# Third stage of a two-layer decoder: GpSimd's products four heads at a time, and VectorE's order around the sums of values and the cross attention's row addition

## The reference

```python
def _L1_attn_ref(x, wq, wk, wv, wo, sink):          # rope, band of 64, 16 heads on 4 key heads
    ...
def _L1_xattn_ref(q, k, v, Wq, bq, Wk, bk, Wv, bv, Wo, bo):
    Q = (q @ Wq.T + bq).reshape(bs, sl, H, HD)       # H = 16 heads of HD = 16
    K = (k @ Wk.T + bk).reshape(bs, sl, H, HD)
    V = (v @ Wv.T + bv).reshape(bs, sl, H, HD)
    score = jnp.einsum('bshd,bsgd->bshg', Q, K)
    weight = jax.nn.softmax(score, axis=-1)
    attn = jnp.einsum('bshg,bsgd->bshd', weight, V).reshape(bs, sl, nf)
    return attn @ Wo.T + bo
def _L1_ffn_ref(hidden_states, ln1_w, ln2_w, Wq, Wk, Wv, Wo, A, B, W_in_base, W_up_base, W_down):
    mod = MOD_SCALE * jnp.tanh(_attention(rmsnorm(h, ln1_w)) @ A)      # causal, 16 heads
    gate_pre = h @ W_in_base.T + mod * (h @ A) @ B                     # h = rmsnorm(hidden, ln2_w)
    return residual + (silu(gate_pre) * (h @ W_up_base.T)) @ W_down.T
```

## Time and profile before

| what | value |
|---|---|
| median of three runs | 3036.44 us |
| the profiled execution, its own time | 3033.89 us |
| its span from first to last instruction | 3032.2 us |
| busy over the span: PE / DVE / ACT / POOL | 2750.8 / 2487.2 / 1954.2 / 2111.9 us |
| third stage, first gather to the end | about 1940 to 3032 us |
| steady turns of the third stage | 24, from 2164.9 to 2885.8 us |
| products q-k, 512 instructions | 358.9 us, 743 ns each |
| products weights-values, 512 instructions | 369.5 us, 760 ns each |

### The profile page before, as it was taken

The page is one execution under the profiler, slowest core; times in us unless marked ns, Lnnn a source line. Parts: engine busy times, 40 slices in busy tenths (PEclk is TensorE's granted clock), DMA queues, the critical chain, the costliest instruction groups (busy, mean ns, idle before and its releaser), DMA issues. The chain is left out here.

```text
span 3032.2 us, 68140 instructions
## 1 busy us (share of the span) xinstructions
PE 2750.8 (91%) x22096; PEld 2295.9 (76%) x22128; DVE 2487.2 (82%) x5452; ACT 1954.2 (64%) x4120; POOL 2111.9 (70%) x2651
## 2 busy tenths in 40 slices
PE   6999999999999999999788499667999999999978
PEld 3888888888888888888555299535777777777767
DVE  6888888888888888888599577468899898989863
ACT  5888878778787877878444155346666666666642
POOL 5897666666666666666468544369888989898870
PEclk9999999999999999999899699768999999999989
DMA  4555444444444444444444399600000000000000
GB/s 144 172 193 169 133 143 139 144 135 146 137 131 153 131 143 132 155 131 128 142 152 146 134 337 333 207 15 18 20 19 27 21 25 24 22 24 22 21 5 11
DMA packets 185881, 340.09 MB, mean 112 GB/s; under 512 B 40668, under 2 KB 104037, under 8 KB 178936
## 3 DMA queue, kind: packets, MB, share of 16 engines
q1 hardware_dynamic: 179448, 319.55, 32.6%
q0 software_dynamic: 6144, 16.79, 1.8%
HBM read 264.68 MB, written 63.19 MB: 108 GB/s over the span
## 5 line engine op out<-in xcount | busy, mean ns | idle before, releaser
L1804 POOL TENSOR_TENSOR l_prod<-l_sco,l_kv 128x256 f32<-128x256 f32 x512 | 369.5, 760 | 36.4 <-DVE l_sco L2311 36.4
L1797 POOL TENSOR_TENSOR l_prod<-l_q,l_kv 128x256 f32<-128x256 f32 x512 | 358.9, 743 | 47.3 <-DVE l_att L2319 47.3
L718 DVE SCALAR_TENSOR_TENSOR a_cq<-a_PQ,a_taps,a_cq 128x504 f32<-128x504 f32 (+2 forms) x384 | 281.7, 734 | 72.7 <-ACT a_cq L584 63.6
L718 DVE SCALAR_TENSOR_TENSOR a_ck<-a_PK,a_taps,a_ck 128x504 f32<-128x504 f32 (+2 forms) x384 | 280.6, 731 | 9.7 <-ACT a_ck L584 0.5
L342 POOL TENSOR_TENSOR a_tq<-a_cq,a_tq 128x512 f32<-128x512 f32 x128 | 165.9, 1296 | 131.2 <-ACT a_tq L590 131.1
L329 POOL TENSOR_TENSOR a_hrs<-a_hve,a_neghalf 128x8 f32<-128x8 f32 x128 | 209.6, 1638 | 25.7 <-DVE a_hve L735 25.2
L485 PE MATMUL a_Y<-a_wo,a_og_parts 128*128 128x256 f32 x1536 | 205.9, 284 | 5.0 <-POOL a_og_parts L336 5.0
L412 PEld LDWEIGHTS a_X<-a_wv,a_xb 128*128 128x128 f32 x1536 | 200.0, 188 | 12.1 <-issue 1.2
L342 POOL TENSOR_TENSOR a_tk<-a_ck,a_tk 128x512 f32<-128x512 f32 x128 | 163.6, 1278 | 62.8 <-ACT a_tk L590 62.8
L412 PE MATMUL a_PQ<-a_x_hi,a_wqk 128*128 (+1 forms) x512 | 194.1, 420 | 12.6 <-issue 11.9
L412 PE MATMUL a_X<-a_wv,a_xb 128*128 128x256 f32 x1536 | 204.2, 282 | 0.8 <-DMA a_xb<-a_x_lo 0.8
(11 more groups left out here) (398 smaller groups left out, 8380.6 us busy)
## 6 DMA issues: line engine op xcount, KB each, us to landing
a_wqk<-qk_parts SPq DMA_DIRECT2D x112, 512.0 KB, 3.4
m_wgu<-gate_up_parts SPq DMA_DIRECT2D x39, 1024.0 KB, 8.1
a_wv<-v_parts SPq DMA_DIRECT2D x56, 512.0 KB, 3.8
a_wg<-g_parts SPq DMA_DIRECT2D x112, 256.0 KB, 3.3
a_wo<-o_parts SPq DMA_DIRECT2D x112, 256.0 KB, 2.9
a_dr<-decays SPq DMA_DIRECT2D x256, 64.0 KB, 2.6
m_hs<-sorted_rows SPq DMA_DIRECT2D x39, 256.0 KB, 7.1
sorted_outs<-m_ys SPq DMA_DIRECT2D x39, 256.0 KB, 7.5
```

The costliest lines, as they stand in the source:

```text
L718: nc.vector.scalar_tensor_tensor(out=acc, in0=src, scalar=taps[p][:, tap + k:tap + k + 1], in1=acc, op0=ALU.mult, op1=ALU.add).then_inc(s_ ...
L1797: nc.gpsimd.tensor_tensor(out=prod[:, h], in0=qv[:, h:h + 1, :].to_broadcast([P, H, HD]), in1=kk, op=ALU.mult).then_inc(S("E_pqk"), 1)
L1804: nc.gpsimd.tensor_tensor(out=prod[:, h], in0=sco[:, h:h + 1, :].to_broadcast([P, HD, H]), in1=vv, op=ALU.mult).then_inc(S("E_pav"), 1)
```

## The change

Three things change in the third stage, and nothing in the first two.

1. products_qk and products_av issue four instructions of 128 x 1024 (four heads) instead of sixteen of 128 x 256. One operand is broadcast over the last heads' axis, as before, and the other one over the four heads. The counts of E_pqk and E_pav follow (4 per tile instead of 16).
2. gather passes the row numbers straight from slots to the indirect DMA; the copy into of_tile, the two small operations and their semaphores are gone.
3. VectorE's list: f_x2lo and E's statistics stand behind the last sum of values; sums 2 and 1 of values stand ahead of m_hidden(1); et_x stands in the next turn, behind the first score sum and ahead of F's arguments.

The core of the diff:

```diff
             def load_kv(t):
                 if t >= 3:
-                    sp.wait_ge(S("E_pav"), H * (t - 2))
+                    sp.wait_ge(S("E_pav"), 4 * (t - 2))
...
-                for h in range(H):
-                    nc.gpsimd.tensor_tensor(out=prod[:, h], in0=qv[:, h:h + 1, :].to_broadcast([P, H, HD]), in1=kk,
-                                            op=ALU.mult).then_inc(S("E_pqk"), 1)
+                for k in range(4):
+                    heads = slice(4 * k, 4 * k + 4)
+                    nc.gpsimd.tensor_tensor(out=prod[:, heads], in0=qv[:, heads, :].unsqueeze(2).to_broadcast([P, 4, H, HD]),
+                                            in1=kk.unsqueeze(1).to_broadcast([P, 4, H, HD]), op=ALU.mult).then_inc(S("E_pqk"), 1)
...
-                for h in range(H):
-                    nc.gpsimd.tensor_tensor(out=prod[:, h], in0=sco[:, h:h + 1, :].to_broadcast([P, HD, H]), in1=vv,
-                                            op=ALU.mult).then_inc(S("E_pav"), 1)
+                for k in range(4):
+                    heads = slice(4 * k, 4 * k + 4)
+                    nc.gpsimd.tensor_tensor(out=prod[:, heads], in0=sco[:, heads, :].unsqueeze(2).to_broadcast([P, 4, HD, H]),
+                                            in1=vv.unsqueeze(1).to_broadcast([P, 4, HD, H]), op=ALU.mult).then_inc(S("E_pav"), 1)
...
             def gather(t):
-                wait_if(pool, S("G_ready"), 2 * t)
                 wait_if(pool, S("G_x"), 2 * t)
-                nc.gpsimd.tensor_tensor(out=ready[:], in0=neghalf[:, 0:1], in1=neghalf[:, 0:1], op=ALU.mult).then_inc(S("G_ready"), 1)
-                nc.gpsimd.tensor_copy(of_tile[:], slots[:, tile(t), :].rearrange("p t k -> p (t k)")).then_inc(S("G_at"), 1)
...
-                                                 bass.IndirectOffsetOnAxis(ap=of_tile[:, k:k + 1], axis=0)).then_inc(S(f"G_in{k}"), 16)
+                                                 bass.IndirectOffsetOnAxis(ap=slots[:, t, k:k + 1], axis=0)).then_inc(S(f"G_in{k}"), 16)
...
-            iterate(dve, [("Et", et_scores(0)), ("Ft", arguments("F")), ("F", statistics("F", "E_x", 1)), ("Et", et_scores(2)),
+            iterate(dve, [("Et", et_scores(0)), ("F", et_x), ("Ft", arguments("F")), ("F", statistics("F", "E_x", 1)), ("Et", et_scores(2)),
...
```

More of the change, by code:

```diff
@@ L1666, in layer_one @@
         got = [sb(f"got{k}", [P, D]) for k in range(2)]
-        of_tile, ready = sb("of_tile", [P, 2], mybir.dt.uint32), sb("ready", [P, 1])
         xT = {k: sb("xT" + k, [P, DC, P]) for k in "DF"}
@@ L1802, in products_av @@
                 vv = kv[t % 3][:, 1, :].rearrange("p (d g) -> p d g", d=HD)
-                for h in range(H):
-                    nc.gpsimd.tensor_tensor(out=prod[:, h], in0=sco[:, h:h + 1, :].to_broadcast([P, HD, H]), in1=vv,
-                                            op=ALU.mult).then_inc(S("E_pav"), 1)
+                for k in range(4):
+                    heads = slice(4 * k, 4 * k + 4)
+                    nc.gpsimd.tensor_tensor(out=prod[:, heads], in0=sco[:, heads, :].unsqueeze(2).to_broadcast([P, 4, HD, H]),
+                                            in1=vv.unsqueeze(1).to_broadcast([P, 4, HD, H]), op=ALU.mult).then_inc(S("E_pav"), 1)
             def gather(t):
-                wait_if(pool, S("G_ready"), 2 * t)
                 wait_if(pool, S("G_x"), 2 * t)
-                nc.gpsimd.tensor_tensor(out=ready[:], in0=neghalf[:, 0:1], in1=neghalf[:, 0:1], op=ALU.mult).then_inc(S("G_ready"), 1)
-                nc.gpsimd.tensor_copy(of_tile[:], slots[:, tile(t), :].rearrange("p t k -> p (t k)")).then_inc(S("G_at"), 1)
-                pool.wait_ge(S("G_ready"), 2 * t + 1)
-                pool.wait_ge(S("G_at"), t + 1)
-                nc.gpsimd.tensor_tensor(out=ready[:], in0=neghalf[:, 0:1], in1=neghalf[:, 0:1], op=ALU.mult).then_inc(S("G_ready"), 1)
                 for k in range(2):
                     nc.gpsimd.indirect_dma_start(got[k][:], None, outs[:, :],
-                                                 bass.IndirectOffsetOnAxis(ap=of_tile[:, k:k + 1], axis=0)).then_inc(S(f"G_in{k}"), 16)
+                                                 bass.IndirectOffsetOnAxis(ap=slots[:, t, k:k + 1], axis=0)).then_inc(S(f"G_in{k}"), 16)
             pool.wait_ge(S("masked"), 4)
@@ L2077, in e_q @@
             def e_q(t):
-                wait_if(act, S("E_pqk"), H * t)
+                wait_if(act, S("E_pqk"), 4 * t)
                 act.wait_ge(S("E_qp"), t + 1)
@@ L2292, in piece @@
                 def piece(t):
-                    wait_if(dve, S("E_pav"), H * t)
-                    dve.wait_ge(S("E_pqk"), H * t + 4 * k + 4)
+                    wait_if(dve, S("E_pav"), 4 * t)
+                    dve.wait_ge(S("E_pqk"), 4 * t + k + 1)
                     nc.vector.reduce_sum(sco[:, 4 * k:4 * k + 4, :], prod[:, 4 * k:4 * k + 4], axis=AX).then_inc(S("E_sc"), 1)
@@ L2317, in piece @@
                     wait_if(dve, S("E_aTp"), t)
-                    dve.wait_ge(S("E_pav"), H * t + 4 * k + 4)
+                    dve.wait_ge(S("E_pav"), 4 * t + k + 1)
                     nc.vector.reduce_sum(att[:].rearrange("p (h d) -> p h d", d=HD)[:, 4 * k:4 * k + 4, :], prod[:, 4 * k:4 * k + 4],
@@ L2385, in _ @@
             dve.wait_ge(S("masked"), 4)
-            iterate(dve, [("Et", et_scores(0)), ("Ft", arguments("F")), ("F", statistics("F", "E_x", 1)), ("Et", et_scores(2)),
+            iterate(dve, [("Et", et_scores(0)), ("F", et_x), ("Ft", arguments("F")), ("F", statistics("F", "E_x", 1)), ("Et", et_scores(2)),
                           ("Et", et_scores(1)), ("Et", et_scores(3)), ("Et", et_shift), ("Dt", divide("D", EB)), ("Et", et_weights),
                           ("M", m_hidden(0)), ("D", d_rope), ("Dn", combine), ("Et", et_values(0)), ("Ft", divide("F", MI)),
-                          ("Dn", statistics("D", "G_x", 2)), ("F", f_x2lo), ("Dt", d_x), ("M", m_hidden(1)),
-                          ("En", statistics("E", "D_x", 1)), ("Et", et_values(2)), ("Et", et_values(1)), ("Ft", ft_gm),
-                          ("Et", et_values(3)), ("D", arguments("D")), ("Ft", ft_gm_lo), ("Md", m_x), ("Et", et_x), ("Et", split_low)])
+                          ("Dn", statistics("D", "G_x", 2)), ("Dt", d_x), ("Et", et_values(2)), ("Et", et_values(1)), ("M", m_hidden(1)),
+                          ("Et", et_values(3)), ("F", f_x2lo), ("En", statistics("E", "D_x", 1)), ("Ft", ft_gm),
+                          ("D", arguments("D")), ("Ft", ft_gm_lo), ("Md", m_x), ("Et", split_low)])
 def decoder(nc, a, x_in, out):
```

## The result

The changed kernel takes 3077.58 us (median of four runs, 3067.49 to 3082.56) against 3037.46 (four runs, 3029.61 to 3044.65): a ratio of 1.0128, interval 1.0105 to 1.0152. It is slower by some 40 us; forecast were 3074 in 3046 to 3110, and slower at 0.83. The profiled execution took 3078.49 us, 3076.7 us of them span.

A forecast was written before the change was run, and what follows sets the result against it. The ring between TensorE and VectorE was taken as the bound: profiled 3033.9 + 34 (steady turns) + 4 (split_low) + 1 (first and last turns) = 3073, set at 3074 us towards the median; range 3046 to 3110.

The forecast's parts named there:

- The ring: Third stage: TensorE and VectorE feeding each other set the 30 us turn; GpSimd is fed and not waited for.
- The length of a product: GpSimd's four-head products: 2.25 us each from start to start, with 2.13 and 2.8 kept as ends.
- The gather sums: VectorE's two gather sums wait for whole GpSimd products in flight; the second ends at 7.8, 2.6 us later.
- L1472 row: Earlier case: a VectorE instruction, median 1.22 us, took 2.82 when issued during GpSimd's 2.35 us L1025.
- Cover and sum: D's sum to TensorE's D values: 1.2 of 2.6 us absorbed, values 1.42 later, turn 31.45, +34 over 24 turns.
- The other moves: Steady turn's reordered sums, E's statistics, et_x and gather: counted as 0, ScalarE's normalisation just hidden by 0.1 us.
- gm_lo: VectorE's L2336, asked at about 19.6, is let through at the first q-k product's end, 19.65.
- rival 2: gm_lo misses the first product's end and waits for the second: +23 to +40, about 3100 us; chance 0.26.
- Once only: Outside steady turns: split_low's additions held up by products, +4 us; first and last turns together +1.
- 1 (no instruction-long wait): Rival: gather sums do not wait for whole products, ring as before, 3031 us; chance 0.12.
- 3: Rival: four-head products cost what four instructions did, 2.8 us, TensorE +3.1 per turn, about 3114 us; chance 0.07.
- 4: Rival: GpSimd is the bound after all, so its lighter work gives -29 to -40, 3000 us; chance 0.05.

The follow-up runs named there:

- Run with reductions: Changed kernel with each gather sum replaced by a one-operand reduction, weighting and addition left out: 3024.59 us, ratio 0.9975.
- two-head run: Changed kernel with products of two heads (8 instructions of 128x512 per run) instead of four: 3031.01 us, ratio 0.9993.

## Why the prediction was right, point by point

- **The ring, and GpSimd off it.** Right. GpSimd does 4 us less per turn and the turn is longer.
- **The length of a product.** 2.25 was a little short: 2.35 beside few VectorE operations and 2.43 beside the gather sums. The upper end, 2.8, is out: two broadcast operands cost little here, 2.35 against the 2.18 and 2.35 of the earlier trace rows.
- **The gather sums.** The step held: the first waits for the second product's end, the second for the third's. The second ends at 8.03 behind the weights multiply, where 7.8 was said; the 0.2 is the first two products, which take 2.35 each from start to start. Run with reductions, the loss is gone, so in a steady turn this was the term, and no other one. One of its two supports was misread: the row addition of 2.84 us did not wait for one product in flight but through four of 0.72, so it is no case of a wait of one instruction, and "at most 0.7" is not so either. Only the L1472 row carried the step.
- **Cover and sum.** D's sum at 11.00 (10.75 said), D's values at 11.06 (10.92; the step from VectorE to TensorE took 0.06, not 0.17), F's maximum 22.58 (22.34), the turn 31.64 (31.45). D's sum ends 2.85 us later than the 8.15 of the prediction's working and D's values start 1.56 later, so the cover is 1.3 us, near the 1.2 said; the two-head run uses 0.8 of it and loses nothing. Over 24 turns +38.8, of which the one turn with the missed end is 1.5, where +34 was said: mis-sized by the product's length.
- **The other moves.** The second hidden half ends at 14.64 (14.5), the last sum of values at 15.77 (15.7), ScalarE's normalisation runs 18.19 to 18.79 (18.2 to 18.8) and the copy at 19.13 waits for TensorE, so it was just hidden. The q-k products run 17.45 to 26.85 (17.4 to 26.5). et_x at 21.44 gained nothing. What I had not asked is whether the old order would have been better with these products: it would have been worse, by gm_lo.
- **gm_lo.** Asked for at 19.59 (19.6), and let through 0.2 us ahead of the product's end in all but one of the steady turns; by the working it was 0.05. That was luck as much as working: the product was longer than said, which gave the room, and the run with it 0.35 us later is rival 2, at 3098 (3100 said).
- **Once only.** The additions of split_low, 2.28 and 2.80 us before, take 2.55 and 4.42 (rows below). The first turn with a weights multiply grows from 32.8 to 36.2 us, near the +4. The first five turns together lose 5.1, the stretch behind the last steady turn gains 3.8 (146.4 to 142.6 us), so +1.3 where +5 was said; too high by about what the steady turns were too low. That the total of 3074 lies so near the 3077.6 is thus partly luck. The rest of the profiled executions' difference, 4.4 us ahead of the first weights multiply, comes from earlier: the first gather already starts 5.3 us later (1945.2 instead of 1939.9), behind stages that the change does not touch.
- **The rivals.** 1 (no instruction-long wait) and 3 are out by the rows above; 4 is out, since a lighter GpSimd gave nothing. 2 happened in one turn of 24.

split_low's additions, the second one in the kernel before by time, then both in the changed kernel by line:

```profile
2032.04 2.80 DVE L2348 TENSOR_TENSOR l_wup<-l_hid,l_wup 128x2048 fp32r<-128x2048 f32 x1
L2343 DVE TENSOR_TENSOR l_win<-l_hid,l_win x1: 2553/2553/2553, 2034.0 to 2034.0; 128x2048 fp32r<-128x2048 f32 x1
L2343 DVE TENSOR_TENSOR l_wup<-l_hid,l_wup x1: 4418/4418/4418, 2036.5 to 2036.5; 128x2048 fp32r<-128x2048 f32 x1
```

## What to carry to other kernels

Before several short GpSimd instructions are joined into one long one, look for VectorE instructions with two SBUF operands that run beside them: each may wait for the whole instruction, and the wait stands in the instruction's own time, not in a list of waits. What that costs is the wait less the cover of whoever needs the result: here 0.8 us more was free and 2.9 us cost 1.6 per turn. Shorten the products, or move the sums to where GpSimd is idle: both took the loss away here. A single SBUF operand would do it too by the run with reductions, but that run left out the weighting, so a kernel that computes the same in that way is not shown. And where a wait of a turn is removed, ask which one is next: several were within a microsecond.
